# An adaLN attention and MLP block: q and k as two float32r parts with heads paired on row tiles, f*f on GpSimd alone, and a new order of work

## The chip, the cores and the metric

The kernel runs on one core of a Trainium2 chip. A time is the device time of one execution in microseconds (us), and the figure to be predicted is the median of several executions. The engines are PE (TensorE), DVE (VectorE), ACT (ScalarE), POOL (GpSimd) and SP (SyncE, which issues every DMA here).

## The reference

For each of 8 batches (512 tokens, 128 features) the block computes a modulated layer norm, attention over 16 heads of 8 dimensions, a gated residual, a second modulated norm, an MLP with weights of +1 and -1, and a second gated residual:

```python
attn = einsum('bhsd,bhtd->bhst', q, k) * hd ** -0.5
x = attn - max(attn, axis=-1)
neg = 1 / (1 - x * (1 - 0.5 * x * (1 - x / 3)))      # x <= 0, so only this branch counts
attn = neg / sum(neg)
x1 = x + ga * (attn @ v @ w_out.T + b_out)
h = relu(s0 * (concat(h2, -h2) @ w0)) * 2            # 256 -> 512, w = where(bool, 1, -1)
h = relu(s1 * (h @ w1)) * 2                          # 512 -> 512
y = x1 + gb * (s2 * (h @ w2))                        # 512 -> 128
```

## The kernel before

The denominator of `neg` is a cubic with one real root, so it is written as f = (s + c) * z, where z is a shifted logit and s = (z + shift)^2. A probability is then 1/sqrt(f*f). For one head (512 queries by 512 keys) the work goes through the engines in this chain:

1. **Logits for the maxima** (`logits`, L486): PE multiplies q by k into `SA`, two PSUM banks of 512 columns, one query tile each. DVE takes the maxima out of them (`maxima`, L749).
2. After four heads (a "quad") PE transposes the maxima (L496), DVE negates them into `ms` (L761), POOL splits them into three bfloat16 parts `mp` (L941 to L949), and SP writes these as extra rows of `QH`. These rows subtract the maximum in the next product.
3. **Scores** (`scores`, L465): PE forms z into `Z`, which has two halves of 1024 columns (two key tiles each).
4. ACT squares each half into `sq` (L557). DVE forms f in `cub` (`from_z`, L737), which frees that half of `Z`.
5. POOL computes f*f (L890), and for three heads in sixteen ACT does it (L567, the string `ON_POOL`). `cub` is a ring of 3 heads. ACT takes 1/sqrt (L582) into `prob`, a ring of 8, two steps later.
6. PE multiplies by v (`with_v`, L510), four heads side by side on column tiles, and ACT copies the sums into `OT`.

q and k come as three bfloat16 parts each. The product of three by three parts takes 72 rows (`NROW`) and the rows for the maximum lie at 96. For batches after the first, DVE copies the product out of PSUM (L816) and POOL makes all parts out of it (L922 to L932).

The 16 heads of a batch are 16 steps of a loop that every engine runs in its own order, written by hand; semaphores tie them together. The rest of the block is placed between the heads by two tables: `MISC` says at which step PE makes which product ("l1_0" to "l1_3" are the 512x512 layer, each of four matmuls in float32), and `EVENTS` places the norms and gates. The offset in an entry says which batch the product belongs to: while batch b is in attention, the MLP of batch b-2 is done, and q and k of batch b+1 are made. A float32 matmul shows in the trace as two instructions, so that "x4" at L435 is two matmuls.

Of the kernel before, what the change touches and what calls it, by code (L numbers as in the profile page):

```python
# [7 lines left out]
BF16 = mybir.dt.bfloat16  # L8
# [54 lines left out]
def short(name, off, step, place=0, point="e"):  # L69
    return name, off, [(step, place, CHUNKS)], (step, point)  # L70


def long_(name, off, step):

    return name, off, [(step, 0, CHUNKS // 2), (step, 1, CHUNKS // 2)], (step + 1, "s")


MISC = [
    short("hT", 1, 0), short("q", 1, 1), short("k", 1, 2), short("h2T", -2, 3),
    short("l0_0", -2, 4), short("l0_1", -2, 5), short("l0_2", -2, 6), short("l0_3", -2, 7), short("v", 1, 8),  # L80
    long_("l1_0", -2, 9), long_("l1_1", -2, 10), long_("l1_2", -2, 11), short("x1", -1, 12), long_("l1_3", -2, 13),
    ("y", -2, [(14, 0, 2), (14, 1, 1), (15, 0, 1)], (15, "e")),
]
MISC_LAST = {
    B - 1: [short("h2T", -2, 0), *(short(f"l0_{m}", -2, m + 1) for m in range(KC)),
            *(long_(f"l1_{m}", -2, m + 5) for m in range(KC)), short("x1", -1, 9), long_("y", -2, 9),
            short("h2T", -1, 12), short("l0_0", -1, 13), short("l0_1", -1, 13), short("l0_2", -1, 14),
            short("l0_3", -1, 14), long_("l1_0", -1, 15)],
    B: [long_("l1_1", -2, 0), long_("l1_2", -2, 6), long_("l1_3", -2, 7), short("x1", -1, 8), long_("y", -2, 9),
        short("h2T", -1, 10)],  # L90
    B + 1: [*(short(f"l0_{m}", -2, m) for m in range(KC)), *(long_(f"l1_{m}", -2, m + 4) for m in range(KC)),
            long_("y", -2, 8)],
}

EVENTS = {
    "den_sq": (7, 1), "den_inv": (8, 0), "att": (8, 1, "pool"), "st2": (13, 0), "mv2": (14, 0), "rs2": (14, 1),  # L100
    "x1n": (15, 0, "pool"), "w2g": (11, 1), "wog": (5, 1), "xbg": (7, 1),
}
# [8 lines left out]
def is_first(b):
    return isinstance(b, int) and b == FIRST


def misc_of(b):
    return MISC_LAST.get(b, MISC) if isinstance(b, int) else MISC


def event(b, name):
    return EVENTS_LAST.get(b, {}).get(name, EVENTS[name]) if isinstance(b, int) else EVENTS[name]  # L120


def live(beta):

    return not isinstance(beta, int) or 0 <= beta < B


def adaln_block(nc, x, w_qkv, w_out, b_out, k0, k1, k2, s0, s1, s2, c, wmod, out):
# [7 lines left out]
    with ExitStack() as ctx:  # L136
# [177 lines left out]
        def bank_of(b, i):

            if is_first(b) and misc_of(b)[i][0] == "k":
                return SA[:, 0, :], None
            if not isinstance(b, int) or (b, i) not in tail:
                return MB[:, :], None
            k = tail.index((b, i))  # L320
            return (SA[:, k % BANKS - 1, :] if k % BANKS else MB[:, :]), k

        def products_at(b, n, points):

            return [(name, b + off, bank_of(b, i)[0]) for i, (name, off, _, (step, point)) in enumerate(misc_of(b))
                    if step == n and point in points and live(b + off)]

        def logits_bank(b, beta, h, qt):

            pair = (TB * h + qt) // 2  # L330
            if is_first(b) and pair % 3:
                return Z[:, pair % 3 - 1, :].rearrange("p (t s) -> p t s", t=2)
            return SA

        def batches(body):

            def run(eng):
                for b in range(FIRST, B + 2):
                    body(b)
            return run  # L340
# [775 lines left out]
```

## Time and profile before

| | |
|---|---|
| median of 3 runs | 837.32 us (834.61 to 837.56) |
| profiled execution | 835.29 us, span of its instructions 833.5 us |
| PE matmuls | 648.3 us busy, 78% of the span |
| DVE | 664.4 us busy, 80% |
| ACT | 620.6 us busy, 74% |
| POOL | 595.3 us busy, 71% |
| mean granted TensorE clock | 0.948 of full speed |

Busy time overlaps itself a little: an instruction of DVE, ACT or PE often starts before the recorded end of the one ahead of it, so the distance between two starts tells more than a duration. "x4" behind a row is a count of instructions merged in it; what stands in brackets behind a row is the idle time of the engine before it and what ended that time.

### The profile page before, as it was taken

What the parts mean: (1) busy time and instruction counts of PE and PEld (TensorE: products, weight loads), DVE (VectorE), ACT (ScalarE), POOL (GpSimd) and SP (SyncE); (2) the same over time, 40 slices, a digit from 0 to 9 for tenths busy, and PEclk for the clock granted to TensorE, in tenths of its full rate; (3) what the DMA queues carried; (4) which work ended last, traced back from release to release, by engine and by line L of the source; (5) the groups of instructions that cost most, each with busy time, mean ns of one, the idle gap of its engine ahead of it and who ended that gap; (6) DMA issues with size and microseconds to landing.
All of it is one profiled execution on the core that took longest, in us unless ns stands there. A gap on an engine that the chain in (4) does not pass through costs nothing.

```text
span 833.5 us, 9550 instructions
## 1 busy us (share of the span) xinstructions
PE 648.3 (78%) x2897; PEld 224.3 (27%) x2897; DVE 664.4 (80%) x785; ACT 620.6 (74%) x541; POOL 595.3 (71%) x507
## 2 busy tenths in 40 slices
PE   3076777777777898779977898679877997996887
PEld 2022111111121333223422342123421342341244
DVE  5389899989997889887998889798997889866120
ACT  1005789889888888698788788698779789889621
POOL 7306887789887967977887967977798677775310
PEclk9968599989999999999999999999999999997999
DMA  2211111210221002210131012210221012000100
GB/s 79 71 60 55 49 38 54 71 56 24 71 65 52 28 28 84 76 41 0 59 94 56 20 39 84 69 37 7 63 80 60 6 42 71 7 8 6 44 22 13
DMA packets 34996, 39.39 MB, mean 47 GB/s; under 512 B 6376, under 2 KB 28160, under 8 KB 34944
## 3 DMA queue, kind: packets, MB, share of 16 engines
q1 hardware_dynamic: 34944, 38.77, 14.7%
q8 instruction: 24, 0.39, 0.2%
q14 instruction: 28, 0.23, 0.1%
HBM read 25.77 MB, written 8.40 MB: 41 GB/s over the span
## 4 chain that ended last, share of the span: by engine, by line
PE 37%; DVE 22%; issue 15%; POOL 14%; ACT 10%; DMA 2%; DVEq 0%; ACTq 0%; SPq 0%; POOLq 0%
PE MB L435 11%; DVE mx L749 10%; DVE cub L737 8%; POOL cub L890 7%; PE Z L465 6%; PE OP L510 5%; PE SA L486 5%; ACT sq L557 4%; ACT prob L582 2%; PE SA L435 2%; POOL rem L925 2%; PE MB L444 2%; PE MB L428 2%; POOL SQ L932 1%; ACT cub L567 1%
## 5 line engine op out<-in xcount | busy, mean ns | idle before, releaser
L890 POOL TENSOR_TENSOR cub<-cub 128x2048 f32<-128x2048 f32 x104 | 373.8, 3597 | 66.5 <-DVE cub L737 66.5
L737 DVE SCALAR_TENSOR_TENSOR cub<-sq,Z 128x1024 f32<-128x1024 f32 x256 | 309.4, 1210 | 48.5 <-ACT sq L557 48.3
L749 DVE TENSOR_REDUCE mx<-SA 128x2 f32<-128x1024 f32 (+1 forms) x277 | 303.1, 1098 | 53.4 <-PE SA L486 51.7
L557 ACT ACTIVATE sq<-Z,shift 128x1024 f32<-128x1024 f32 x256 | 281.3, 1114 | 69.8 <-PE Z L465 68.9
L582 ACT ACTIVATE prob<-cub 128x2048 f32<-128x2048 f32 x128 | 244.7, 1912 | 35.9 <-POOL cub L890 35.9
L486 PE MATMUL SA<-KH,QH 96*128 96x512 bf16 x492 | 165.9, 400 | 89.8 <-DVE mx L749 42.8
L465 PE MATMUL Z<-QH,KH 128*128 128x512 bf16 x512 | 162.5, 400 | 68.0 <-DVE cub L737 66.0
L510 PE MATMUL OP<-prob,Vq 128*16 128x512 f32 x1024 | 140.1, 622 | 3.1 <-ACT OT L612 3.1
L435 PE MATMUL MB<-hid,W 128*128 128x512 f32 x216 | 101.2, 593 | 0.9 <-ACT hid L600 0.9
L486 PEld LDWEIGHTS SA<-KH,QH 96*128 96x128 bf16 x492 | 42.0, 100 | 216.5 <-issue 108.2
L465 PEld LDWEIGHTS Z<-QH,KH 128*128 128x128 bf16 x512 | 35.7, 99 | 234.7 <-DVE cub L737 161.6
L600 ACT ACTIVATE hid<-MB,sv 128x512 f32<-128x512 f32 x54 | 37.0, 686 | 52.3 <-PE MB L435 43.3
L941 POOL TENSOR_SCALAR mp<-ms 16x128 bf16<-16x128 f32 x32 | 9.2, 288 | 80.0 <-DVE ms L761 80.0
L435 PEld LDWEIGHTS MB<-hid,W 128*128 128x128 f32 x216 | 40.6, 189 | 37.6 <-issue 30.7
L567 ACT ACTIVATE cub<-cub 128x2048 f32<-128x2048 f32 x24 | 45.8, 1909 | 0.0
L428 PE MATMUL MB<-h2T,W 128*128 128x512 f32 x54 | 32.9, 696 | 0.0
L510 PEld LDWEIGHTS OP<-prob,Vq 128*16 128x16 f32 x1024 | 17.4, 95 | 56.6 <-issue 53.5
L860 POOL TENSOR_TENSOR rs<-mv,eps 128x4 f32<-128x4 f32 x16 | 3.2, 197 | 31.1 <-DVE mv L790 26.1
L444 PEld LDWEIGHTS MB<-W2G,hid 128*128 128x128 f32 x192 | 23.9, 192 | 2.2
L444 PE MATMUL MB<-W2G,hid 128*128 128x128 f32 x192 | 24.0, 275 | 0.0
L612 ACT ACTIVATE OT<-OP 128x512 f32<-128x512 f32 x32 | 18.9, 591 | 5.4 <-PE OP L510 5.4
L833 DVE TENSOR_TENSOR y<-SA,x1k 128x512 f32<-128x512 f32 x2 | 1.4, 690 | 26.2 <-PE SA L444 26.2
(125 smaller groups left out, 508.6 us busy)
## 6 DMA issues: line engine op xcount, KB each, us to landing
QH<-parts_q SPq DMA_DIRECT2D x96, 96.0 KB
KH<-parts_k SPq DMA_DIRECT2D x32, 288.0 KB
nd<-OT SPq DMA_DIRECT2D x128, 32.0 KB
parts_q<-SQ SPq DMA_DIRECT2D x24, 128.0 KB
parts_k<-SK SPq DMA_DIRECT2D x24, 128.0 KB
xa<-L_attn_x SPq DMA_DIRECT2D x8, 256.0 KB, 8.7
xb<-L_attn_x SPq DMA_DIRECT2D x8, 256.0 KB, 8.9
out<-y SPq DMA_DIRECT2D x8, 256.0 KB, 2.2
```

What stands on the lines that cost most here:

```text
L428: mm = nc.tensor.matmul(bank, W0[:, m * P:(m + 1) * P], h2T[:, :], start=True, stop=True)
L435: mm = nc.tensor.matmul(bank, W1[:, kc, m * P:(m + 1) * P], hid[0][:, kc, :], start=(kc == 0), stop=(kc == KC - 1))
L444: mm = nc.tensor.matmul(bank4[:, t, :], hid[1][:, kc, t * P:(t + 1) * P], W2G[:, kc, :], start=(kc == 0), stop=(kc == KC - 1))
L465: mm = nc.tensor.matmul(Z[:, h, t * S:(t + 1) * S], KH[:, n, k0_:k0_ + P], QH[:, n, :], start=True, stop=True)
L486: nc.tensor.matmul(logits_bank(b, beta, hh, qt)[:, qt % 2, :], QH[0:MROW, hh, qt * P:(qt + 1) * P], KH[0:MROW, hh, :], start=True, stop=Tr ...
L510: mm = nc.tensor.matmul(OP[32 * j:32 * j + 2 * HD, :], Vq[:, tb, hh, :, :].rearrange("p d a -> p (d a)"), prob[:, hh % P_RING, tb * S:(tb ...
L557: nc.scalar.activation(sq[:, h, :], Z[:, h, :], ACT.Square, bias=shift[:, 0:1]).then_inc(s_sq, 1)
L567: nc.scalar.activation(f, f, ACT.Square).then_inc(s_fa, 1)
L582: nc.scalar.activation(prob[:, m % P_RING, :], cub[:, (H * beta + m) % F_RING].rearrange("p a n -> p (a n)"), RSQRT).then_inc(s_p, 1)
L737: nc.vector.scalar_tensor_tensor(cub[:, (H * b + n) % F_RING, h, :], sq[:, h, :], CUB_ADD, Z[:, h, :], ALU.add, ALU.mult).then_inc(s_cv, 1)
L749: nc.vector.tensor_reduce(mx[:, g % 2, j * TB + qts[0]:j * TB + qts[-1] + 1], logits_bank(b, beta, QUAD * g + j, qts[0])[:, qts[0] % 2:qts ...
L890: nc.gpsimd.tensor_tensor(ff, ff, ff, ALU.mult).then_inc(s_fp, 1)
```

## The change

- **q and k are split into two float32r parts** instead of three bfloat16 ones (`PARTS = 2`, `QH` and `KH` of type F32R). ACT writes the first part out of PSUM with a copy, DVE the second with one subtraction (`split`, L690). POOL has no part in it. The maxima are split in the same way by two DVE instructions (L679, L681), without `ms`.
- **Two heads share a matmul pair.** One head's rows lie on partitions 0 to 36, the other's on 64 to 100. The unit of a step is no longer one head with four key tiles but two heads with two key tiles ("group"); each of the two matmuls of a pair addresses its own half of the array's rows. There are as many matmuls as before: 4 for scores and 4 for logits in a step.
- **POOL computes every f*f** (128 instead of 104). Both rings, `cub` and `prob`, have 4 places.
- **The order of all engines is written anew.** In DVE's step stand: cubic of half 0, maxima, cubic of half 1, maxima. PE has three places for other products in a step ("a", "c", "d"), and a product of layer 1 is cut into single matmuls. Logits run 7 steps ahead of the scores (before: 8). POOL's f*f of a step now stands in that same step and no longer in the next one.
- At the start POOL clears no more of `QH` and `KH`; six small memsets and four DMAs fill the constant rows.

```diff
-    short("hT", 1, 0), short("q", 1, 1), short("k", 1, 2), short("h2T", -2, 3),
-    short("l0_0", -2, 4), short("l0_1", -2, 5), short("l0_2", -2, 6), short("l0_3", -2, 7), short("v", 1, 8),
-    long_("l1_0", -2, 9), long_("l1_1", -2, 10), long_("l1_2", -2, 11), short("x1", -1, 12), long_("l1_3", -2, 13),
-    ("y", -2, [(14, 0, 2), (14, 1, 1), (15, 0, 1)], (15, "e")),
+    ("hT", 1, [(0, "a", 4)]), ("q", 1, [(0, "c", 4)]), ("k", 1, [(1, "c", 4)]),
+    ("l1_0", -2, [(3, "a", 1), (3, "c", 1), (3, "d", 1), (4, "a", 1)]),
+    ("l1_1", -2, [(4, "c", 1), (4, "d", 1), (5, "a", 1), (5, "c", 1)]),
+    ("l1_2", -2, [(6, "a", 1), (6, "c", 1), (6, "d", 1), (7, "a", 1)]),
+    ("x1", -1, [(8, "a", 4)]),
+    ("l1_3", -2, [(9, "a", 1), (9, "c", 1), (9, "d", 1), (10, "a", 1)]),
+    ("y", -2, [(10, "c", 1), (10, "d", 1), (11, "a", 1), (11, "c", 1)]),
+    ("v", 1, [(12, "c", 4)]), ("h2T", -1, [(13, "c", 4)]),
+    ("l0_0", -1, [(14, "a", 4)]), ("l0_1", -1, [(14, "c", 4)]),
+    ("l0_2", -1, [(15, "a", 4)]), ("l0_3", -1, [(15, "c", 4)]),
...
-        QH = sb("QH", [P, H, S], BF16)
-        KH = sb("KH", [P, H, S], BF16)
-        prob = sb("prob", [P, P_RING, TB * S])
-        cub = sb("cub", [P, F_RING, 2, HALF])
+        QH = sb("QH", [P, 2 * NQ, S], F32R)
+        KH = sb("KH", [P, 2 * NQ, S], F32R)
+        prob = sb("prob", [P, RING, TB * S])
+        cub = sb("cub", [P, RING, 2, HALF])
...
+                for e in range(2):
+                    rows = slice(64 * e, 64 * e + K_Z)
+                    mm = nc.tensor.matmul(Z[:, h, e * S:(e + 1) * S], KH[rows, 2 * g + r, keys], QH[rows, 2 * g + r, :],
+                                          start=True, stop=True)
...
+            m = s + AHEAD
+            scores(s + 1, 0)
+            if m % QUAD == 0 and m >= QUAD:
+                logits(m, 0, (1,))
+            misc("a")
+            logits(m, 1, (0, 1))
+            with_v(s)
+            scores(s + 1, 1)
+            misc("c")
+            maxima_across(m)
+            logits(m + 1, 0, (0,) if (m + 1) % QUAD == 0 and m + 1 >= QUAD else (0, 1))
+            misc("d")
...
+            square_of(s + 1, 0)
+            take("a")
+            if at(s, "den_inv", -1, b, n):
...
+            square_of(s + 1, 1)
+            take("c")
+            take_numerators(s)
...
+            prob_of(s - BEHIND)
```

How PE's order changes, at a step with layer 1 (`MB<-hid,W`). Before, four of its matmuls stand in one step, in two blocks of two:

```order
L465 MATMUL Z<-QH,KH 128x512 x2
L435 MATMUL MB<-hid,W 128x512 x2
L486 MATMUL SA<-KH,QH 128x512 x2
L435 MATMUL MB<-hid,W 128x512 x2
L465 MATMUL Z<-QH,KH 128x512 x2
L486 MATMUL SA<-KH,QH 128x512 x2
L510 MATMUL OP<-prob,Vq 16x512 x4
```

In the changed kernel a step of the same kind (step 3 of a batch) holds three, each by itself:

```order
L427 MATMUL Z<-QH,KH 128x512 x2
L387 MATMUL MB<-hid,W 128x512
L446 MATMUL SA<-KH,QH 128x512 x2
L467 MATMUL OP<-prob,Vq 16x512 x4
L427 MATMUL Z<-QH,KH 128x512 x2
L387 MATMUL MB<-hid,W 128x512
L446 MATMUL SA<-KH,QH 128x512 x2
L387 MATMUL MB<-hid,W 128x512
```

The matmuls of a step are as many as before but for the layer's, of which one has moved to a neighbouring step.

POOL before, from f*f of a batch's last head to the third head of the next:

```order
L890 TENSOR_TENSOR cub<-cub 128x2048
L922 TENSOR_SCALAR SQ<-rem 128x512
L925 TENSOR_TENSOR rem<-rem,SQ 128x512
L929 TENSOR_SCALAR SQ<-rem 128x512
L932 TENSOR_TENSOR SQ<-rem,SQ 128x512
L890 TENSOR_TENSOR cub<-cub 128x2048
L922 TENSOR_SCALAR SK<-rem 128x512
L925 TENSOR_TENSOR rem<-rem,SK 128x512
L929 TENSOR_SCALAR SK<-rem 128x512
L932 TENSOR_TENSOR SK<-rem,SK 128x512
L890 TENSOR_TENSOR cub<-cub 128x2048
```

POOL in the changed kernel, at the fullest place of a batch (steps 9 to 12); at steps 2 to 4 it has nothing but f*f:

```order
L774 TENSOR_TENSOR rs<-mv,eps 128x4
L776 TENSOR_TENSOR rs<-rs,half 128x4
L808 TENSOR_TENSOR cub<-cub 128x2048
L814 TENSOR_SCALAR xn<-xa,mv,rs 128x128 x4
L808 TENSOR_TENSOR cub<-cub 128x2048
L774 TENSOR_TENSOR rs<-mv,eps 128x4
L776 TENSOR_TENSOR rs<-rs,half 128x4
L814 TENSOR_SCALAR x1n<-x,mv,rs 128x128 x4
L808 TENSOR_TENSOR cub<-cub 128x2048 x2
```

The eight instructions of the splits are gone, and both normalisations stand in neighbouring steps.

## Rows read from the trace of the kernel before

**Rows 1.** The chain that ended last, by engine (the page)
```profile
PE 37%; DVE 22%; issue 15%; POOL 14%; ACT 10%; DMA 2%; DVEq 0%; ACTq 0%; SPq 0%; POOLq 0%
```
**Rows 2.** Stretches (batches 0, 1, 4, 7): length, PE, PEld, DVE, ACT, POOL, clock, DMA, GB/s
```profile
64.70:146.00 81.30, 58.28 (x228) 13.05 (x228) 77.32 (x85) 64.44 (x52) 64.38 (x47) 0.85 0.14 46
146.00:228.90 82.90, 60.92 (x284) 14.19 (x284) 79.03 (x94) 71.55 (x59) 70.25 (x57) 0.94 0.17 54
...
414.30:506.70 92.40, 76.69 (x361) 27.68 (x360) 80.26 (x94) 76.72 (x68) 74.31 (x64) 0.98 0.16 52
...
691.30:776.60 85.30, 71.67 (x326) 25.55 (x325) 63.58 (x68) 76.49 (x69) 59.84 (x44) 0.94 0.12 31
```
**Rows 3.** Waits of DVE in batch 4: us in total, times, longest
```profile
DVE mx L749 <- PE SA L486: 6.9, 10, 1.4
DVE cub L737 <- ACT sq L557: 4.7, 5, 2.3
```
**Rows 4.** Timeline of PE over a step with layer 1
```profile
467.45 1.88 PE L435 MATMUL MB<-hid,W 128*128 128x512 f32 x4
469.17 0.60 PE L486 MATMUL SA<-KH,QH 96*128 96x512 bf16 x2
...
471.32 0.59 PE L465 MATMUL Z<-QH,KH 128*128 128x512 bf16 x2
471.75 0.60 PE L486 MATMUL SA<-KH,QH 96*128 96x512 bf16 x2
472.28 1.05 PE L510 MATMUL OP<-prob,Vq 128*16 128x512 f32 x8
473.26 0.60 PE L465 MATMUL Z<-QH,KH 128*128 128x512 bf16 x2
```
**Rows 5.** Timeline of DVE where it never waits
```profile
325.19 0.27 DVE L761 TENSOR_SCALAR ms<-SA 16x128 f32<-16x128 f32 x1
325.39 1.32 DVE L749 TENSOR_REDUCE mx<-SA 128x1 f32<-128x512 f32 x2
326.63 1.21 DVE L737 SCALAR_TENSOR_TENSOR cub<-sq,Z 128x1024 f32<-128x1024 f32 x1
...
328.89 1.21 DVE L737 SCALAR_TENSOR_TENSOR cub<-sq,Z 128x1024 f32<-128x1024 f32 x1
```
**Rows 6.** Timeline of ACT, no wait
```profile
327.62 1.11 ACT L557 ACTIVATE sq<-Z,shift 128x1024 f32<-128x1024 f32 x1
328.61 1.91 ACT L582 ACTIVATE prob<-cub 128x2048 f32<-128x2048 f32 x1
```
**Rows 7.** Groups of POOL instructions: busy us, mean ns, idle before
```profile
L890 POOL TENSOR_TENSOR cub<-cub 128x2048 f32<-128x2048 f32 x104 | 373.8, 3597 | 66.5 <-DVE cub L737 66.5
L897 POOL TENSOR_SCALAR xn<-xa,mv,rs 128x128 f32<-128x128 f32 x28 | 21.9, 793 | 0.1
L862 POOL TENSOR_TENSOR rs<-rs,half 128x4 f32<-128x4 f32 x16 | 16.5, 1032 | 1.3
L943 POOL TENSOR_TENSOR mrem<-ms,mp 16x128 f32<-16x128 f32 x32 | 13.3, 417 | 2.7
L932 POOL TENSOR_TENSOR SK<-rem,SK 128x512 bf16<-128x512 f32 x8 | 9.4, 1172 | 0.7
L929 POOL TENSOR_SCALAR SK<-rem 128x512 bf16<-128x512 f32 x8 | 4.9, 618 | 0.6
```
**Rows 8.** Timeline of ACT behind POOL's splits, batch 2
```profile
254.38 1.91 ACT L582 ACTIVATE prob<-cub 128x2048 f32<-128x2048 f32 x1 [2.74 <-POOL cub L890]
```
**Rows 9.** Timeline of the start
```profile
6.29 3.51 POOL L873 MEMSET KH<- 128x4096 f32 x1
6.37 7.17 DVE L681 TENSOR_SCALAR xn<-xa,mv,rs 128x128 f32<-128x128 f32 x4
...
41.41 1.01 PE L486 MATMUL SA<-KH,QH 96*128 96x512 bf16 x2 [19.06 <-DMA KH<-parts_k]
```
**Rows 10.** Timeline of PE at the end
```profile
785.35 5.18 PE L510 MATMUL OP<-prob,Vq 128*16 128x512 f32 x32 [2.17 <-ACT OT L612]
```

More of the change, by code:

```diff
@@ L7 @@
 F32 = mybir.dt.float32
-BF16 = mybir.dt.bfloat16
+F32R = mybir.dt.float32r
 U8 = mybir.dt.uint8
@@ L62 @@
-N_P = squares("P", H - 1)
-N_A = squares("A", H - 1)
+R_PROD = 32
+R_MAX = 33
+K_LOG = 33
+K_Z = 37
+GROUPS = B * H
+RING = 4
+AHEAD = 7
+BEHIND = 2
+AV_BEHIND = 5
+LOADS = 6
+FIRST = -1
 CHUNKS = 4
 assert CHUNKS == KC == TB
[L69 to L78, printed above, removed]
-    short("hT", 1, 0), short("q", 1, 1), short("k", 1, 2), short("h2T", -2, 3),
-    short("l0_0", -2, 4), short("l0_1", -2, 5), short("l0_2", -2, 6), short("l0_3", -2, 7), short("v", 1, 8),
-    long_("l1_0", -2, 9), long_("l1_1", -2, 10), long_("l1_2", -2, 11), short("x1", -1, 12), long_("l1_3", -2, 13),
-    ("y", -2, [(14, 0, 2), (14, 1, 1), (15, 0, 1)], (15, "e")),
-]
@@ L84 @@
[L84 to L93, printed above, removed]
@@ L111, in is_first @@
[L111 to L120, printed above, removed]
-def live(beta):
-    return not isinstance(beta, int) or 0 <= beta < B
+MAIN = [
[10 rows of a table added]
+]
+MISC = {b: MAIN for b in range(FIRST, B - 1)}
+MISC[B - 1] = [
[9 rows of a table added]
+]
+MISC[B] = [
[6 rows of a table added]
+]
+MISC[B + 1] = [
+    ("l1_2", -2, [(0, "a", 2), (0, "c", 2)]), ("l1_3", -2, [(1, "a", 2), (1, "c", 2)]),
+    ("y", -2, [(2, "a", 4)]),
+]
@@ L312, in adaln_block @@
-        BANKS = 3
+        order = [(b, i) for b in range(FIRST, B + 2) for i, m in enumerate(MISC[b]) if live(b + m[1])]
+        late = [(b, i) for b, i in order if b >= B]
+        banks = [MB[:, :], SA[:, 0, :], SA[:, 1, :]]
         def bank_of(b, i):
-            if is_first(b) and misc_of(b)[i][0] == "k":
+            if b == FIRST and MISC[b][i][0] == "k":
                 return SA[:, 0, :], None
[L318 to L340, printed above, removed]
@@ new lines, in logits @@
+                if heads[0] == 0:
+                    if m == 0 and u == 0:
+                        pe.wait_ge(s_gate, 1)
+                        pe.wait_ge(s_rows, 4 * 16)
+                    if m % QUAD == 0 and u == 0:
+                        pe.wait_ge(s_qk[g], (beta + 1) * LOADS * 16)
+                    need(pe, s_mx, unit_before(m, u))
+                else:
+                    need(pe, s_mp, m // QUAD)
+                for e in heads:
+                    rows = slice(64 * e, 64 * e + K_LOG)
+                    nc.tensor.matmul(unit_bank(m, u)[:, e, :], QH[rows, 2 * g + r, qt * P:(qt + 1) * P],
+                                     KH[rows, 2 * g + r, :], start=True, stop=True).then_inc(s_a, 1)
@@ new lines, in maxima_across, with with_v @@
+            def maxima_across(m):
+                if 0 <= m < GROUPS and m % QUAD == QUAD - 1:
+                    pe.wait_ge(s_mx, 4 * (m + 1))
+                    nc.tensor.transpose(SA[0:QUAD * TB, 1, 0:P], mx[:, m // QUAD % 2, :], ident[:, :]).then_inc(s_mt, 1)
+            def with_v(s):
+                quad, tb = (s - AV_BEHIND) // QUAD, (s - AV_BEHIND) % QUAD
+                if not 0 <= quad < B * NQ:
+                    return
+                g = quad % NQ
+                if tb % 2 == 0:
+                    pe.wait_ge(s_p, QUAD * quad + tb + 2)
@@ L537, in _ @@
             pe_setup(pe)
-            batches(lambda b: pe_batch(pe, b))(nc.tensor)
+            steps(lambda s: pe_step(pe, s))
         def act_setup(act):
@@ L654, in _ @@
             act_setup(act)
-            batches(lambda b: act_batch(act, b))(nc.scalar)
+            steps(lambda s: act_step(act, s))
         def dve_setup(dve):
@@ new lines, in dve_step @@
+            cubic(s, 0)
+            take_maxima(m)
+            if m % QUAD == 0 and m >= QUAD:
+                maxima(m, 0, (0,))
+                maxima(m, 0, (1,))
+            else:
+                maxima(m, 0, (0, 1))
+            split(b, n)
+            if s > FIRST * H:
+                take((s - 1) // H, (s - 1) % H, "cd")
+            cubic(s, 1)
+            maxima(m, 1, (0, 1))
+            take(b, n, "a")
+            misc()
+            if b == FIRST and n == 3:
+                dve_gates(dve)
@@ L1089, in _ @@
             sp_setup(sp)
-            batches(lambda b: sp_batch(sp, b))(nc.sync)
+            steps(lambda s: sp_step(sp, s))
             sp.wait_ge(s_out, 16 * B)
```

836 lines of the change are left out of this document (348 added, 488 removed), and 15 rows, old and new, of the table MISC.

## The prediction

> **What bounds the kernel now.** I read the chain that ended last first. It gives PE 37%, DVE 22%, POOL 14% and ACT 10% [rows 1]: no engine alone, the work passes from one to another. So I cut the span at the first cubic of each batch. Batches 2 to 6 take 92.3 to 92.9 us each, batches 0 and 1 take 81.3 and 82.9, batch 7 takes 85.3 [rows 2]; together 711.9 of 833.5 us, with 64.7 ahead and 56.9 behind. In a full batch DVE is the busiest engine, 80.3 of 92.4 us [rows 2], and its waits are 6.9 us for logits from PE and 4.7 for squares from ACT [rows 3]. These 12 us are what can be won in a batch; DVE's four passes of 1024 columns in each step are the floor.
>
> **What a step costs each engine.** Where DVE never waits, a cubic and a maxima pass follow each other in 2.26 us (326.63 to 328.89) [rows 5], so a step of two halves is 4.53. Where PE never waits (clock full), a pair of bfloat16 matmuls takes 0.43, two float32 layer matmuls 1.72 (one 0.86), logits before the v product 0.53, the v product 0.98 [rows 4]. A step's attention (four pairs and the v product) is then 3 x 0.43 + 0.53 + 0.98 = 2.8 us; with four layer matmuls it is 2.8 + 3.43 = 6.23, and the trace has 6.25 from 467.45 to the same place a step later (473.26 + 0.44 for the pair that stands there) [rows 4]. Such a step is PE's, not DVE's. ACT needs two squares at 0.99 and one root at 1.91 less the same overlap, 3.8 in all [rows 6].
>
> Now a table of 16 steps, the larger of DVE and PE in each. DVE: 4.53, and 0.6 for each PSUM pass of 512 columns (half of the 1.24 from 325.39 to 326.63), 0.33 where a quad ends (0.20 for the small operation, 0.12 for splitting a pass in two: 325.39 to 326.63 is 1.24 against 1.13) [rows 5], 1.0 for each norm's statistics (my estimate, from their being eight short passes). That sums to 78.9. The larger of the two sums to 85.6, since layer 1 lifts four steps to 6.2 and y lifts one. The batch takes 92.4; the 6.8 left over is POOL. At steps 2 and 3 it makes all parts of q and k, for each two operations of 1.17 and two of 0.62 [rows 7], 3.6 us on top of an f*f of 3.6, so 7.2 in a step of 5; then ACT waits for f*f, 2.74 us once in batch 2 [rows 8], and cannot square meanwhile. The table plus this explains the whole batch, which is why I trust it for the new order.
>
> **The change, part by part.**
>
> *POOL.* Gone are q's and k's splits, 7.1 us in a batch, and four times the splits of the maxima, two of 0.42 and two shorter, about 1.4 each, 5.7 us [rows 7]. Added are 3 f*f of 3.6, 10.8. The sum hardly moves; the place does. Its new crowd is steps 9 to 11: three f*f (10.7), two normalisations of four 0.79 passes (6.4), two roots of 1.03 and a 0.2 (2.5) [rows 7], 19.6 us against about 16 us of steps by the table below. It falls some 4 us behind. f*f now stands in its own step, and the ring has 4 places: from a group's last cubic to the cubic that wants its place are three steps and a pass, 14.7 us; f*f, root and square take 3.6 + 1.9 + 1.1, so over 7 us of lag are free. Cover holds; with it gone the stall would be like today's 6.8.
>
> *ACT* loses 3 f*f of 1.8 and gets two copies of 0.5; about 4 us less in a batch, but steps 14, 15 and 0 carry two products each, 5.0 to 5.4.
>
> *DVE* gets a second small operation per quad, 0.2 and a wait on itself, another 0.2: 0.73 where it was 0.33. Sum 80.5. The floor rises 1.6 us per batch.
>
> *PE.* Layer 1 is spread: 3 matmuls in steps 3, 4, 6, 9, 10, so 2.8 + 2.57 = 5.4 (5.6 with a transpose or y) instead of 6.23. Layer 0 stands in pairs at 14 and 15, 4.5.
>
> *The pair.* No row shows a float32r matmul or one of 64 rows. From below: float32 goes two instructions of 0.43 each per 512 columns, bfloat16 one of 0.215 [rows 4]; if two row halves run together at bfloat16's pace, a pair is 0.22. The v product shows that tiles do overlap: eight float32 instructions in 0.98, not in 3.4 [rows 4]. From above: no overlap and float32's 0.43 for each, 0.86. I take 0.43, today's value, which is either half of the two advantages.
>
> With that the step maxima of the new table are 5.4, 5.9, 5.1, 5.4, 5.6, 5.3, 5.4, 4.9, 5.1, 6.0, 5.5, 4.6, 5.1, 5.9, 5.0, 5.0: 85.0. With a pair of 0.22 it is 82.7, with 0.64 it is 90.3, with 0.86 it is 100.4. The row of turns weighs too: going to column tiles costs PE 0.53 - 0.43 = 0.1, coming back 0.98 - 0.86 = 0.12 [rows 4]. If row tiles cost the same, each of 30 products that now stand between attention pairs costs 0.2 more, which counts in the five or six steps that are PE's: 85.0 becomes 87.9. I take 86.
>
> The Trainium skill, TensorEngine Tiling (Array Packing), Key Properties, says that a change of tiling mode drains the engine. The trace agrees for column tiles, by the 0.1 above; that it does so for row tiles no row shows. By the rule the full batches are the 87.9 and the time 805, the upper part of my own case.
>
> *Batches.* Batch 0 has no x1, y, second norm: DVE 78.3, ACT's late step 0.9, and the low clock of 0.85 [rows 2] about 2, as now: 81. Batch 1: 82. Batches 2 to 6: 5 x 86 = 430. Batch 7: nine steps at 48.4; the last seven have no maxima and go by ACT and POOL at 4.2 to 5.4, 33: 81.5. Sum 674.5 against 711.9: -37.4.
>
> *Start.* DVE's first normalisation takes 7.17 us while POOL clears KH [rows 9]; the four passes are 0.8 each elsewhere at most [rows 7], and POOL still has a memset of Vq there: 4 to 5 us less. POOL's splits leave the way to the first logits, 14 maxima passes of 1.13 instead of 16 come ahead of the first cubic, but layout and loads (six instead of four per quad, issued one after the other) take some back. First logits are now at 41.4 [rows 9]. I take -7, between -2 and -12.
>
> *End.* PE's last v products end at 790.5 (785.35 + 5.18) [rows 10], 14 us after the last cubic. The new table puts 12 layer matmuls and y (10.3 + 3.7) and the v products (4 x 1) of two steps before x1, 17 to 18: +3, between 0 and +5.
>
> Sum: 833.5 - 37.4 - 7 + 3 = 792; the profiled execution (835.3) lies 1.8 above its span and the median 2 above that execution: **796**.
>
> **Rivals.**
>
> *The pair is cheaper than I take it* (0.15): 0.22 and no cost of turns, 82.7 a batch; 5 x 3.3 = 16 less, start at -10: 777.
>
> *PE's clock falls* (0.10). With cheap pairs PE works less. At 58.3 busy of 81.3 the clock was 0.85, at 76.7 of 92.4 it was 0.98 [rows 2]. A full batch with pairs of 0.22 has 57 to 60 us of PE work, a share like batch 0's. Then PE's steps of 4.6 to 5.4 stretch where the clock is at its lower level; some 4 us in each of five batches: 816.
>
> *The new crowd on POOL or a late row for the maximum stalls* (0.06): half of today's 6.8 in each of 7 batches, 820.
>
> *The pair costs 0.86* (0.14, ends on the other side). Row halves that wait for each other, at float32's pace: batches of 85, 90, 5 x 100.4, 91 are 768, so +56 in place of -37: 889. It decides from a pair of about 0.7: there a full batch is back at 92.4. For it: two float32 instructions never go faster than 0.43 here. Against it: the overlap of column tiles.
>
> *It comes to the same* (0.03): a pair between 0.64 and 0.7.
>
> **How the numbers follow.** My own case (796, from 780 to 810) has 0.52. Range: it takes in the cheap pair from 770 on and clock and stall up to 832; the slower case and a little on each side are left out, together 0.2. A change under 0.5% (4 us, the spread of the three runs) cannot be told from none. Faster: 0.52 + 0.15 + 0.10 + 0.06 = 0.83; same 0.03; slower 0.14.
>
> **What would show it.** Full batches of 85 to 88 between first cubics; DVE over 90% busy in them; a pair's distance on PE near or under 0.43, and pieces of layer 1 with 0.1 around them if turns cost; no wait of ACT for f*f over 1 us; first cubic at 58; no layer step over 6 us. I am wrong if pairs show 0.6 or more, if the clock in full batches is under 0.9, or if DVE waits at the quad's end for PE's transpose or a row's DMA.

## The result, and the profile after

The changed kernel takes **886.05 us** (median of 4 runs, 880.64 to 891.17) where the one before takes 836.71 on the same chip: a ratio of **1.0593 [1.0523, 1.0662]**, slower. The forecast was 796, faster. The profiled execution takes 884.32 us and spans 882.3.

The page gives the chain that ended last, by engine; it answers to [rows 1]:

```profile
PE 60%; DVE 18%; issue 11%; ACT 7%; DMA 3%; SPq 1%; POOL 0%; DVEq 0%; ACTq 0%; POOLq 0%
```

PE had 37% of the chain and now has 60%; POOL had 14% and now has none. So POOL was relieved, and PE took more than it gave. The same cut at the first cubics as in [rows 2], for batches 0, 1, 4 and 7 (length, then busy time of PE, PEld, DVE, ACT, POOL, the granted clock, DMA share, GB/s):

```profile
60.50:148.70 88.20, 71.80 (x234) 23.96 (x234) 79.28 (x88) 59.82 (x50) 60.33 (x26) 1.00 0.15 47
148.70:245.10 96.40, 85.60 (x300) 27.55 (x296) 81.19 (x98) 69.99 (x62) 70.42 (x39) 0.84 0.15 48
...
437.90:533.10 95.20, 86.50 (x360) 29.95 (x360) 81.66 (x99) 73.36 (x68) 72.65 (x44) 0.87 0.16 50
...
731.20:814.10 82.90, 74.36 (x313) 25.30 (x313) 62.64 (x69) 70.60 (x64) 66.74 (x35) 0.90 0.07 21
```

The eight batches take 88.2, 96.4, 97.4, 95.4, 95.2, 100.7, 97.4 and 82.9, together 753.6 against 711.9. DVE's work in batch 4 has grown by 1.4 us as forecast, but PE's by 9.8, and the clock, 0.98 before, is 0.87. (The 1.00 of batch 0 is no reading, and the 0.84 of batch 1 only half of one: this trace holds no clock records ahead of 203 us, and a stretch without records counts as full. In batch 0 the first and the fifth matmul of a v product start 826 ns apart and not 440, which is the lower level, and `e11_tail` below, with the same batch 0, has the records.) Start and tail: the first cubic comes at 60.5 instead of 64.7, and 68.2 us follow the last cubic instead of 56.9. So +41.7, -4.2 and +11.3 make the +48.8 us.

What DVE and ACT wait for in batch 4 (us in total, times, longest) [rows 3]:

```profile
DVE mx L668 <- PE SA L446: 12.5, 14, 1.5
...
ACT sq L507 <- PE Z L427: 20.3, 14, 2.8
```

Both wait for PE. The wait for squares is gone from DVE in this batch, and f*f stopped nobody: in the profile page's groups prob has no idle time ahead of it, where [rows 8] had 2.74 in one place, and POOL itself now stands idle for cubics:

```profile
L808 POOL TENSOR_TENSOR cub<-cub 128x2048 f32<-128x2048 f32 x128 | 460.6, 3601 | 175.3 <-DVE cub L657 174.3
...
L518 ACT ACTIVATE prob<-cub 128x2048 f32<-128x2048 f32 x128 | 243.8, 1904 | 0.0
```

PE's timeline inside a step with layer 1 at the full clock, against [rows 4]. Here and below a distance is taken from one start to the next, as the rows' own durations overlap:

```profile
464.38 1.13 PE L387 MATMUL MB<-hid,W 128*128 128x512 f32 x2
465.43 0.51 PE L427 MATMUL Z<-QH,KH 37*128 37x512 f32 x2
465.87 1.12 PE L387 MATMUL MB<-hid,W 128*128 128x512 f32 x2
466.93 0.49 PE L446 MATMUL SA<-KH,QH 33*128 33x512 f32 x2
467.35 1.05 PE L467 MATMUL OP<-prob,Vq 128*16 128x512 f32 x8
468.33 0.49 PE L427 MATMUL Z<-QH,KH 37*128 37x512 f32 x2
```

A pair lasts from 465.43 to 465.87, 0.44: the two row halves run together, and the pair is the 0.43 that I took. A layer matmul lasts from 465.87 to 466.93, 1.06, where it was 0.86. And a stretch 8 us earlier reads so, with the same instructions:

```profile
453.73 1.91 PE L467 MATMUL OP<-prob,Vq 128*16 128x512 f32 x8
455.57 0.79 PE L427 MATMUL Z<-QH,KH 37*128 37x512 f32 x2
...
457.81 2.07 PE L387 MATMUL MB<-hid,W 128*128 128x512 f32 x2
459.82 0.79 PE L446 MATMUL SA<-KH,QH 33*128 33x512 f32 x2
```

This is the lower of the two clock levels, 1.2 GHz: the v product takes 1.84 instead of 0.98, a layer matmul 2.01 instead of 1.06. In this batch the records show that level from 448.9 to 462.6, from 493.3 to 496.7 and from 520.6 to 527.4, 23.9 us; over batches 2 to 6 it is 27.3, 23.9, 23.9, 37.5 and 23.9 us. Before, it was 3.4 us in each.

### The profile page after: what moved, and what is told of

Same layout as the page of the kernel before. It is cut to its first block, busy times and chain, and to the rows that moved or that the text cites. A ratio compares the mean times of both kernels' runs of the same rounds, so it can differ in the third digit from the quotient of the medians.

```text
span 882.3 us, 9519 instructions
## 1 busy us (share of the span) xinstructions
PE 745.2 (84%) x2897; PEld 264.9 (30%) x2897; DVE 667.6 (76%) x814; ACT 590.6 (67%) x531; POOL 581.2 (66%) x350
## 4 chain that ended last, share of the span: by engine, by line
PE 60%; DVE 18%; issue 11%; ACT 7%; DMA 3%; SPq 1%; POOL 0%; DVEq 0%; ACTq 0%; POOLq 0%
PE MB L387 14%; PE OP L467 13%; PE SA L446 10%; PE Z L427 8%; DVE mx L668 8%; DVE cub L657 6%; PE MB L396 3%; PE MB L380 3%; PE MB L361 3%; ACT sq L507 3%; ACT prob L518 2%; PE SA L387 2%; ACT hid L544 2%; DMA KH<-parts_k 1%; DMA QH<-mp 1%
## 5 line engine op out<-in xcount | busy, mean ns | idle before, releaser
L808 POOL TENSOR_TENSOR cub<-cub 128x2048 f32<-128x2048 f32 x128 | 460.6, 3601 | 175.3 <-DVE cub L657 174.3
L446 PE MATMUL SA<-KH,QH 33*128 33x512 f32 x502 | 167.1, 594 | 70.3 <-DVE mx L668 50.0
L467 PE MATMUL OP<-prob,Vq 128*16 128x512 f32 x1024 | 177.8, 774 | 0.0
L427 PE MATMUL Z<-QH,KH 37*128 37x512 f32 x512 | 155.1, 584 | 25.8 <-DVE cub L657 23.3
L387 PE MATMUL MB<-hid,W 128*128 128x512 f32 x216 | 133.2, 707 | 1.1 <-ACT hid L544 0.6
L446 PEld LDWEIGHTS SA<-KH,QH 33*128 33x128 f32 x502 | 63.6, 224 | 220.1 <-DVE mx L668 111.0
L427 PEld LDWEIGHTS Z<-QH,KH 37*128 37x128 f32 x512 | 59.8, 223 | 217.9 <-issue 118.5
L824 POOL COPY Vq<-Vn 128x128 f32<-128x128 f32 x32 | 9.6, 303 | 30.4 <-DVE Vn L708 30.3
L814 POOL TENSOR_SCALAR x1n<-x,mv,rs 128x128 f32<-128x128 f32 x28 | 22.0, 798 | 0.7
L814 POOL TENSOR_SCALAR xn<-xa,mv,rs 128x128 f32<-128x128 f32 x28 | 22.0, 798 | 0.1
```

Of the source, the lines that this page charges most:

```text
L387: mm = nc.tensor.matmul(bank, W1[:, kc, m * P:(m + 1) * P], hid[0][:, kc, :], start=(kc == 0), stop=(kc == KC - 1))
L427: mm = nc.tensor.matmul(Z[:, h, e * S:(e + 1) * S], KH[rows, 2 * g + r, keys], QH[rows, 2 * g + r, :], start=True, stop=True)
L446: nc.tensor.matmul(unit_bank(m, u)[:, e, :], QH[rows, 2 * g + r, qt * P:(qt + 1) * P], KH[rows, 2 * g + r, :], start=True, stop=True).then ...
L467: mm = nc.tensor.matmul(OP[32 * j:32 * j + 2 * HD, :], Vq[:, tb, hh, :, :].rearrange("p d a -> p (d a)"), slot[:, tb % 2, j % 2, :], start ...
L808: nc.gpsimd.tensor_tensor(ff, ff, ff, ALU.mult).then_inc(s_fp, 1)
```

## Experiments

Three suspects stood after the result: the turns between tiled and untiled matmuls, the format of q and k, and the granted clock. A fourth, the tail's order, is a matter by itself.

The mean clock given with a run says less than its time. A trace's clock records begin somewhere between 16 and 203 us, and what lies ahead of them counts as full: the profiled executions have them from 203 us in the changed kernel, 26 in `e1_full`, 47 in `e2_full_bf16`, 120 in `e3_tile_bf16`, 17 in `e4_two` and `e5_twice`, 67 in `e6_rows64`, 143 in `e7_full65` and 16 in `e11_tail`. Two executions of `e7_full65` that both took 834.21 us read 0.936 and 0.864. So the comparisons below rest on times and on batches that the records cover.

### Full array or tiles, four or two bytes

`e1_full` lets each score or logit matmul use the whole height of the array:

```diff
-                    rows = slice(64 * e, 64 * e + K_Z)
+                    rows = slice(0, 128)
...
-                    rows = slice(64 * e, 64 * e + K_LOG)
+                    rows = slice(0, 96)
```

> The changed kernel, but each matmul of a pair takes all rows of the array (128 for scores, 96 for logits; QH and KH are cleared at the start), still float32r. It mixes the two heads of a pair, so what it computes is not the reference's; counts, order and sizes are the same. Theory A (row tiles: each turn between half arrays and the full array costs 0.2 us and the clock falls because of them): full batches 84 to 89 us, clock 0.95 or more, time 795 to 825. Rival B (float32r: the matmuls are short, and that lets the clock fall): full batches 92 or more, clock under 0.90, time 865 or more. Rival C (the new order of PE): as B, but with PE's waits for DVE unchanged at a full clock.

Measured: 830.1 us, 0.9956 [0.9935, 0.9977] of the kernel before; clock 0.944. Without tiles the full batches take 87.2 to 88.4 us with none of it at the lower level, where the changed kernel's took 95 to 101. The time lies 5 us over theory A's range and far under B's.

`e2_full_bf16` is that with `F32R = mybir.dt.bfloat16` for QH, KH and the parts.

> As e1_full, and with all of q, k and the maximum's parts in bfloat16 (the same number of rows and matmuls; DMAs move half the bytes; rounding differs and heads are mixed). Theory A (row tiles): as e1_full within 1%, 795 to 825. Rival B (float32r): only here does the time come down to 790 to 825, while e1_full stays over 865. Rival C (order): over 865 like the others.

Measured: 796.89 us, 0.9546 [0.9527, 0.9565]; clock 0.961. That lies in theory A's range and in rival B's, but 4% under `e1_full`, so the format costs something too.

`e3_tile_bf16` has the changed kernel's tiles and bfloat16's two bytes.

> The changed kernel with row tiles as it is, but q, k and the maximum's parts in bfloat16 (less exact numbers, same work). Theory A (row tiles): the turns stay at 0.2 us less what the shorter weight load saves, the clock stays under 0.92, time 855 to 885. Rival B (float32r): clock 0.95, time 790 to 825.

Measured: 824.98 us, 0.9882 [0.9863, 0.9902]; clock 0.869. The clock is theory A's and the time rival B's, so both hold a share.

The four together, in us:

```
              float32r   bfloat16
row tiles        886        825
full array       830        797
```

Both parts of the change in PE's work cost time: tiles 56 us with one format and 28 with the other, float32r 61 and 33. Of float32r's cost 9 and 10 us lie ahead of the first cubic (60.5 against 51.6, 71.7 against 61.5, with twice the bytes to move); the rest is in the batches. Of tiles the table shows less than they cost there, because the full-array kernels also clear QH and KH at the start and reach the first cubic 11.2 and 9.9 us later: from the first to the last cubic tiles take 67 us more with float32r (753.6 against 686.2) and 38 with bfloat16 (703.9 against 666.0). The table of steps that gave 85.0 for a full batch was right: in `e2_full_bf16`, with the changed kernel's order, batches 2 to 6 take 84.9, 84.9, 85.0, 85.2 and 84.8. Batch 4 of it and then of `e3_tile_bf16`:

```profile
394.40:479.40 85.00, 75.57 (x361) 26.57 (x360) 80.61 (x98) 72.59 (x67) 72.45 (x44) 1.00 0.13 37
```
```profile
406.00:498.30 92.30, 83.14 (x360) 23.99 (x360) 81.15 (x98) 72.83 (x67) 72.42 (x44) 0.82 0.12 34
```

The same instructions in the batch but for the rows that they use: 7.6 us more of PE's time, at 0.82 and not at 1.00. The full array again, around one layer matmul:

```profile
431.16 0.60 PE L428 MATMUL Z<-QH,KH 128*128 128x512 bf16 x2
431.60 1.02 PE L388 MATMUL MB<-hid,W 128*128 128x512 f32 x2
432.46 0.60 PE L447 MATMUL SA<-KH,QH 96*128 96x512 bf16 x2
```

The layer matmul is back at 0.86 (431.60 to 432.46). Between tiles it took 1.06 with four bytes and with two. So 0.2 is the price of two turns. The row is 0.11 longer (1.13 instead of 1.02), which leaves 0.09 behind it; that the 0.11 is the matmul's own weight load is my guess. A bfloat16 pair in tiles lasts 0.32 next to such a matmul, in full 0.43. Tiles save 0.11 on a pair and pay 0.2 on the piece beside it. A layer matmul and the pair behind it together, at the full clock, take 1.29 in `e2_full_bf16` (431.60 to 432.89), 1.32 in `e1_full` (435.26 to 436.58), 1.38 in `e3_tile_bf16` (447.06 to 448.44) and 1.49 in the changed kernel (464.38 to 465.87).

### Fewer turns

`e4_two` takes the changed kernel and joins the pieces of layer 1 and y in twos:

```diff
-    ("l1_0", -2, [(3, "a", 1), (3, "c", 1), (3, "d", 1), (4, "a", 1)]),
+    ("l1_0", -2, [(3, "a", 2), (3, "c", 2)]),
```

> The changed kernel with layer 1 and y in pieces of two instead of one (10 pieces fewer in a full batch). If each turn costs 0.2 us on PE and PE ends the step, a full batch loses 1 to 2 us: 875 to 882. If the cost of a turn is small beside the clock's fall, within 0.5% of the changed kernel or slower, for blocks of 1.7 us come back: 884 to 895.

Measured: 940.02 us, 1.126 [1.1238, 1.1283]; clock 0.727. A plain miss, above both forecasts. At 2.4 GHz two matmuls together do take 1.92, pair to pair, instead of twice 1.06:

```profile
490.11 1.98 PE L387 MATMUL MB<-hid,W 128*128 128x512 f32 x4
492.03 0.50 PE L446 MATMUL SA<-KH,QH 33*128 33x512 f32 x2
```

So the turns were saved. The clock took more than that, batch 4:

```profile
463.70:570.90 107.20, 95.56 (x366) 35.75 (x362) 81.83 (x99) 73.28 (x66) 71.80 (x44) 0.76 0.14 44
```

The lower level covers 44 to 64 us of a full batch, where it was 24 to 38; batches 0 and 1 take 88.2 and 94.1, where the changed kernel's took 88.2 and 96.4. Over the span the clock of 0.727 is to be held against the 0.784 of `e11_tail`, whose records are whole too, and not against the changed kernel's 0.886. After this run turns alone could not be the story: what is won on them is lost several times over when the clock falls.

### What the clock follows

`e5_twice` gives the tiles of `e3_tile_bf16` twice the work, each score and logit matmul issued twice:

```diff
-                for e in range(2):
+                for e in (0, 1, 0, 1):
```

> e3_tile_bf16 with every score and logit matmul issued twice into the same place (same result, double work on half-array tiles). Theory A1 (the clock falls because overlapping tiles leave the array with little work): the clock rises from 0.869 to 0.94 or more, and the time stays within 2% of 825 or even falls, though PE has about 14 us more to do in a batch at full clock. Theory A2 (half-array tiles as such hold the clock down, or PE is the bound anyhow): clock 0.87 or less, time 860 or more.

Measured: 882.43 us, 1.0565 [1.0513, 1.0617]. Neither theory fits whole: the time is A2's, but in the full batches the lower level shrinks to between 3.4 and 17 us, as A1 has it. They still take 93 to 99 us, since PE has 91.66 us of work in batch 4. Batches 0 and 1 are at the lower level for 82 and 61 us. More work in tiles brings the clock back only where there is a lot of it, and pays for it.

`e6_rows64` lets the scores of `e3_tile_bf16` use all 64 rows of their half, zeros in the added ones (the logits stay at 33):

```diff
-                    rows = slice(64 * e, 64 * e + K_Z)
+                    rows = slice(64 * e, 64 * e + 64)
```

> e3_tile_bf16 with the scores on all 64 rows of each half array instead of 37 (rows 37 to 63 are zero; logits stay at 33; QH and KH are cleared at the start, which costs some 3 to 5 us). If the number of rows in use sets the clock, it rises to 0.93 or more and the time falls to 805 or less; if the time in which matmuls run does, clock 0.87 and 825 to 832.

Measured: 817.84 us, 0.9792 [0.974, 0.9844], between the two forecasts. Lower level 10 to 14 us in a full batch instead of 10 to 34; batches 0 and 1 take 81.4 and 84.5 instead of 83.4 and 90.2. Batch 4:

```profile
403.20:492.50 89.30, 76.37 (x360) 22.61 (x360) 80.98 (x98) 72.90 (x67) 72.41 (x44) 0.92 0.13 35
```

There is no matmul more, and none is shorter at the full clock (a layer matmul 1.06, a pair beside it 0.32, in both): only rows. Outside the batches two memsets that clear QH and KH are new, and with them the first cubic comes at 60.3 instead of 51.6. So the eight batches win 17.6 us (686.3 against 703.9) and the kernel 7.

`e7_full65` cuts the full array of `e2_full_bf16` to 65 rows, in the logits as in the scores:

```diff
-                    rows = slice(0, 128)
+                    rows = slice(0, 65)
```

> e2_full_bf16 (heads mixed, no tiles) with 65 rows in each score and logit matmul instead of 128 and 96. If the number of rows in use sets the clock, it falls from 0.961 to 0.92 or less and the time rises over 810; if the time in which matmuls run does, clock 0.96 and 793 to 801.

Measured: 834.21 us, 1.0004 [0.998, 1.0029]. Turns did not come back: at the full clock a layer matmul takes 0.86 and a pair 0.43 as before, and three of the five full batches take 84.8 to 85.2. The two others take 86.6 and 89.3, with 3.4 and 10.2 us at the lower level. Batches 0 and 1 take 96.1 and 95.3 where they took 81.4 and 81.7. Batch 1 of `e2_full_bf16` and then of this run:

```profile
142.90:224.60 81.70, 63.05 (x295) 15.59 (x294) 79.44 (x97) 69.56 (x61) 70.17 (x39) 0.96 0.12 36
```
```profile
158.30:253.60 95.30, 82.42 (x300) 21.12 (x296) 80.89 (x98) 69.73 (x61) 70.27 (x39) 0.71 0.11 31
```

Some 37 us hang on how many rows the same matmuls occupy. One thing is not held still: the rows taken away also held the second head's numbers. In `e6_rows64` the rows added hold nothing but zeros.

### Each head apart, and what zeros do

`e8_apart` keeps the changed kernel's order and two bfloat16 parts, and gives each head its own block of columns: parts in rows 0 to 31, the maximum and constants in 96 to 99, zeros between. Scores use 100 rows, logits 96, no tiles:

```diff
-                    rows = slice(64 * e, 64 * e + K_Z)
-                    mm = nc.tensor.matmul(Z[:, h, e * S:(e + 1) * S], KH[rows, 2 * g + r, keys], QH[rows, 2 * g + r, :],
+                    hh = QUAD * g + 2 * r + e
+                    mm = nc.tensor.matmul(Z[:, h, e * S:(e + 1) * S], KH[0:100, hh, keys], QH[0:100, hh, :],
```

> The changed order with two bfloat16 parts, but each head in a column block of its own (rows 0 to 31 the parts, 96 to 99 maximum and constants, zeros between), so that no matmul is on a half array; it computes the reference. Theory A (tiles bring turns and the low clock): pairs at 0.43, no turns, clock 0.96, full batches 84 to 86, time 793 to 805. Rivals B and C (type, order): 825 or more.

Measured: 813.09 us, 0.9734 [0.9681, 0.9787], between theory A's range and the rivals'. Batch 4:

```profile
408.30:493.30 85.00, 75.55 (x360) 26.57 (x360) 80.59 (x99) 72.57 (x68) 72.44 (x44) 1.00 0.13 37
```

The full batches are `e2_full_bf16`'s to 0.2 us. The spans differ by 17.6 us, and these lie outside: the first cubic is at 69.3 instead of 61.5 (the clearing holds POOL until 15.2 us), batches 0 and 1 take 85.5 and 83.5 (+5.9, with 41 and 17 us at the lower level), batch 7 takes 2.7 more and the tail 1.0.

`e10_ones` puts ones instead of zeros in QH, `memset(QH[:, :, :], 1.0)`.

> This is the kernel of the separate column blocks with one value changed: rows 32 to 95 of QH hold ones instead of zeros, those of KH stay zero, so every product is the same number. The batches 0 and 1 of that kernel spend 41 and 17 us at the lower clock level and the later ones none. Theory one, the granted clock follows the rows and columns that a matmul occupies and not what stands in them: the same 813 us within 0.4 per cent and the same two batches at the lower level. Theory two, zeros count as rest: with ones in one operand the lower level shrinks in batches 0 and 1 to under half, and the time falls by 4 to 6 us, to 807 to 809.

Measured: 812.57 us, 0.9709 [0.9652, 0.9766]. The lower level: 31 (in the part that the records cover, from 74 us on) and 17 us in batches 0 and 1, none in batches 2 to 6, and 10 in batch 7, as in `e8_apart`. The time is the same within the intervals; the first theory holds in this. The products were zero in both, so data whose products are not zero is not tried here.

### The order of the tail, and of the start

`e11_tail` is the changed kernel with only this altered:

```diff
 MISC[B] = [
-    ("l1_1", -2, [(0, "a", 2), (0, "c", 2)]), ("l1_2", -2, [(1, "a", 2), (1, "c", 2)]),
-    ("l1_3", -2, [(2, "a", 2), (2, "c", 2)]), ("y", -2, [(3, "a", 2), (3, "c", 2)]),
-    ("x1", -1, [(8, "a", 4)]), ("h2T", -1, [(11, "c", 4)]),
+    ("l1_1", -2, [(0, "a", 2), (0, "c", 2)]), ("l1_2", -2, [(5, "a", 2), (5, "c", 2)]),
+    ("l1_3", -2, [(6, "a", 2), (6, "c", 2)]),
+    ("x1", -1, [(8, "a", 4)]), ("y", -2, [(9, "a", 2), (10, "a", 2)]), ("h2T", -1, [(11, "c", 4)]),
```

> This is the changed kernel (886 us) with the tail's order alone altered: layer 1 parts 2 and 3 of batch 6 stand behind the last products with v, and y of batch 6 behind x1 of batch 7. The changed kernel's tail is 68.2 us against 56.9 before. If the order of these matmuls is the reason, x1 begins 5 to 8 us earlier and the time is 878 to 881 us. If the lower clock level of the tail's layers is the reason, the tail keeps 66 us or more and the time stays within 2 us of 886.

Measured: 879.76 us (875.18 to 890.54), 1.0505 [1.0426, 1.0583] of the kernel before, where the changed kernel had 1.0593. The two intervals overlap, so what the order does is read from the tails of the two traces. The changed kernel's tail on PE, last cubic at 814.1:

```profile
835.12 1.05 PE L467 MATMUL OP<-prob,Vq 128*16 128x512 f32 x8
843.48 2.05 PE L369 MATMUL SA<-woG,nd 128*128 128x128 f32 x8 [7.31 <-issue]
851.05 1.09 PE L373 MATMUL SA<-ident,x1n 128*128 128x128 f32 x4 [5.52 <-DVE x1n L745]
853.10 2.05 PE L380 MATMUL MB<-h2T,W 128*128 128x512 f32 x2 [0.96 <-ACT h2T L538]
854.94 3.62 PE L380 MATMUL SA<-h2T,W 128*128 128x512 f32 x4
858.35 1.11 PE L380 MATMUL MB<-h2T,W 128*128 128x512 f32 x2
```

and `e11_tail`'s, last cubic at 818.1:

```profile
829.09 1.91 PE L467 MATMUL OP<-prob,Vq 128*16 128x512 f32 x16 [1.59 <-ACT prob L518]
830.93 7.13 PE L387 MATMUL SA<-hid,W 128*128 128x512 f32 x16
840.79 1.13 PE L369 MATMUL MB<-woG,nd 128*128 128x128 f32 x8 [2.73 <-issue]
841.76 5.36 PE L396 MATMUL SA<-W2G,hid 128*128 128x128 f32 x32
846.96 0.60 PE L373 MATMUL SA<-ident,x1n 128*128 128x128 f32 x4
848.52 1.10 PE L380 MATMUL MB<-h2T,W 128*128 128x512 f32 x2 [0.96 <-ACT h2T L538]
849.45 1.88 PE L380 MATMUL SA<-h2T,W 128*128 128x512 f32 x4
851.17 1.02 PE L380 MATMUL MB<-h2T,W 128*128 128x512 f32 x2
```

x1 begins 22.7 us behind the last cubic instead of 29.4, and the whole tail is 56.9 us instead of 68.2. The order gives 6.7 of the 11.3. The clock gives a share too: the two holes of 7.31 and 5.52 us in which PE had nothing are now filled in good part with batch 6's work, PE goes into batch 7's layers at 2.4 GHz and not at 1.2, and from the first product of layer 0 to the last it takes 2.65 us (848.52 to 851.17) instead of 5.25 (853.10 to 858.35). That is 2.6 of the remaining 4.6; the other 2 I have not traced. This execution's batches happened to take 3.8 us more than the changed kernel's, so the spans show 7.3 of the 11.3.

`e9_order` puts the same tail into `e8_apart`, and in the start computes POOL's first root ahead of the clearing, four bytes at a time:

```diff
+            root_of(pool, 0, mv1, rs1, s_ve1, s_rs1)
+            nc.gpsimd.memset(QH[:, :, :].bitcast(F32), 0.0).then_inc(s_one, 1)
+            nc.gpsimd.memset(KH[:, :, :].bitcast(F32), 0.0).then_inc(s_one, 1)
```

> This is the kernel of the separate column blocks (813.09 us; two bfloat16 parts) with two orders changed and nothing else. In the tail, layer 1 and y of batch 6 stand behind the last products with v and around x1 instead of ahead of them: theory one says that the tail of 68.6 us is long because those matmuls hold up the last products (they end at 22 us behind the last cubic, at 14 us in the kernel before), so x1 comes 5 to 8 us earlier. In the start, POOL computes the first root of the variance ahead of the clearing of QH and KH and clears four bytes at a time, which the trace of the kernel before shows at half the time: the first cubic should come 10 to 16 us earlier than 69.3 us. Together 790 to 798 us. Rival: the end is set by the layers of batch 7 at the lower clock level and by waits for DMAs, and moving work of batch 6 only fills gaps differently; then the tail stays within 2 us and the time is 798 to 803.

Measured: **794.56 us**, 0.9488 [0.9419, 0.9558], the fastest of all here. The first cubic is at 60.5 (8.8 earlier, not 10 to 16), the batches take 85.5, 85.2, four of 85.0 to 85.2, 84.8 and 80.1, and the tail 57.2.

## Why the prediction was wrong

**What bounds a batch, DVE, ACT, POOL: right.** The new table of steps holds to 0.2 us where the clock stays up and nothing turns: 85.0 forecast (its sixteen numbers as printed add up to 85.2) for a full batch, 84.8 to 85.2 measured in `e2_full_bf16`, `e8_apart` and `e9_order`. POOL's stall went without a successor, as forecast.

**The pair: right.** 0.43 to 0.44 beside a layer matmul, 0.33 to 0.34 where two pairs follow each other. The rivals with 0.22 and 0.86 are both out. The rival on the other side gave nearly the measured time (889) by a mechanism that did not occur.

**The turns: named, taken too low.** The working gave 87.9 for a full batch if row tiles cost what column tiles cost, and I took 86. They cost that, 0.2 per piece. If the working's 87.9 holds, the term is 9.5 us too small over five batches. The Trainium skill, TensorEngine Tiling (Array Packing), Key Properties, says that a change of tiling mode drains the engine; the trace agrees, by the 1.06 instead of 0.86, and its 805 was the better sum, if still far off. `e4_two` shows that it is not the main term.

**The clock: the step that failed.** I had it as a rival at 0.10, tied to cheap pairs, with "some 4 us in each of five batches", and took the clock of the own case as that of before, in batch 0 "about 2, as now". Batches 2 to 6 take 486.1 us; at 87.9 they would take 439.5. The other 46.6 us, 9.3 in a batch, go with 136.5 us at the lower level, in which PE's work takes twice as long. This split is a sum and not a measurement, since no run has the changed kernel at the full clock throughout. A straight line through batches 2 to 6 of its trace and of `e11_tail`'s (23.9 to 37.5 us at the lower level, 94.9 to 100.7 long) leads to 86.7 for a batch with none, an estimate well outside its points; by it turns would be 4 us and the clock 52. The clock is the main term either way. Batches 0 and 1 take 88.2 and 96.4 instead of 81 and 82. `e11_tail`, whose batches 0 and 1 are the same program, has their records:

```profile
60.70:148.90 88.20, 71.83 (x234) 23.96 (x234) 79.27 (x89) 59.83 (x50) 60.33 (x26) 0.50 0.15 47
148.90:244.40 95.50, 83.33 (x298) 26.50 (x294) 80.99 (x97) 70.09 (x61) 71.24 (x39) 0.59 0.16 49
```

Batch 0 is wholly at 1.2 GHz, batch 1 for 78.5 us. `e2_full_bf16`, without tiles and with two-byte parts, runs the same two batches in 81.4 and 81.7 us.

The wrong thought behind it was to tie the clock to PE's busy time. [Rows 2] invited it: 58.3 of 81.3 us with 0.85, 76.7 of 92.4 with 0.98. The runs do not follow it: batch 4 is 91% busy at 0.87 in the changed kernel, 90% at 0.82 in `e3_tile_bf16`, 89% at 1.00 in `e2_full_bf16`. These three lines alone would not settle it, since the lower level itself makes PE busy for longer. The clean test is in two pairs of runs in which the matmuls are as many and, at the full clock, as long, and only their rows differ: from `e2_full_bf16` to `e7_full65` (128 and 96 rows to 65) batch 1 goes from 0.96 to 0.71, and from `e3_tile_bf16` to `e6_rows64` (scores from 37 rows to 64) batch 4 goes from 0.82 to 0.92. The Trainium skill, TensorE: Matmul & The Clock Gate, What's actually happening, lets the busy-ness of the engine set the clock ratio; these pairs say that it is not busy time alone. What was shown is that the granted clock also goes with the rows that the matmuls occupy, be there zeros in them or ones in one operand. What in the rows does it (the array's part in use, or what is read for it) no run here separates, and why `e4_two` falls so much further than the changed kernel stays open.

**The start: near.** 60.5 instead of 57.7; DVE's normalisation fell from 7.17 [rows 9] to 1.53, a little more than the 4 to 5 us forecast, and the first logits come at 36.86 instead of 41.41. With the two-byte parts of `e3_tile_bf16` the first cubic is at 51.6, so the four-byte ones cost 9 us here; whether by their bytes or by their matmuls is not separated.

**The end: mis-sized.** +11.3 where I took +3 with a bound of +5. I counted the matmuls ahead of x1 as PE's work, 17 to 18 us, and not that the last v products stand between them in PE's order and wait for root and relu in ACT's; they ended at 22 us. And the lower clock level in batch 7's layers was not in the sum at all (`e11_tail`: 6.7 us for the order, 2.6 for the clock in layer 0).

Against the forecast span of 792 the account is: full batches +56.1 (turns 9.5, clock 46.6, with the split worked out as above), batches 0 and 1 +21.6, batch 7 +1.4, start +2.8, end +8.3. Together +90.2; measured +90.3.

## What to carry to other kernels

Do not alternate row tiles with full-height matmuls one by one: a turn there and back costs 0.2 us per piece, more than the 0.11 that a bfloat16 pair in tiles saves. Pairs that stand together save more (0.23 against 0.43), but `e4_two` shows that grouping can lose more by the clock than it wins, so read the clock as well. And before making matmuls smaller, price PE's work at the lower clock level too: read the granted clock of the stretch you change, and ask whether the new matmuls still occupy the array, since here padding with rows of zeros alone made the eight batches 17.6 us faster (`e6_rows64` 686.3, `e3_tile_bf16` 703.9), half of which the clearing of those rows took back at the start. Keep the last stages' independent work for the holes in which PE would wait: it shortened the tail by 11 us twice, and the lower level in the tail went from 17.1 to 3.4 us (`e11_tail`) and from 20.5 to 3.5 (`e9_order` against `e8_apart`).

Last, look at where a trace's clock records begin before you compare mean clocks: two traces of one program can differ by 0.07 in it at the same time.

## What the runs showed of the hardware

- Two float32r matmuls on the two row halves run at the same time; a pair of 512 columns costs 0.33 to 0.34 us back to back (changed kernel, 476.03 to 476.37) and 0.43 to 0.44 next to a full-height matmul, a bfloat16 pair 0.23 and 0.32 (`e3_tile_bf16`).
- On the full array a bfloat16 pair takes 0.43 (`e2_full_bf16`) and a float32r pair ahead of a layer matmul 0.54 to 0.57 (`e1_full`, 431.74 to 432.28 and 434.69 to 435.26); a layer matmul and such a pair together take 1.32 against 1.29.
- A float32 matmul of 512 columns between row-tiled ones takes 1.06 us (changed kernel, `e3_tile_bf16`) instead of 0.86 (`e2_full_bf16`) at 2.4 GHz.
- 65 instead of 128 and 96 rows in the same untiled matmuls (`e7_full65`, `e2_full_bf16`): 834 instead of 797 us, and a batch 0 of 96.1 instead of 81.4.
- 64 instead of 37 rows in the scores' tiles, the added ones all zeros (`e6_rows64`, `e3_tile_bf16`): 61.5 instead of 99.0 us at the lower level over batches 2 to 6, and the eight batches 17.6 us shorter.
- Joining pieces in twos, fewer turns and no more work (`e4_two`): 263 instead of 137 us at the lower level over batches 2 to 6, and 54 us slower.
